# Graph-transformer kernel on one core: node rows kept in SBUF, three row buffers in the edge stage, seam flags moved

## The reference, cut to what matters

```python
h = maximum(layernorm(x), 0)
for l in range(2):
    k, q, v = typed_linear(h, ntype, Wk[l] / Wq[l] / Wv[l])          # per node
    a = (rel_apply(k[src], etype, Watt) * q[dst]).sum(-1) * pri / sqrt(16)
    alpha = segment_softmax(a, dst)                                 # 8 heads
    agg = segment_sum(alpha * rel_apply(v[src], etype, Wmsg), dst)
    out = silu(typed_linear(agg, ntype, Wa[l]))
    h = layernorm(out * sigmoid(skip[ntype]) + h * (1 - sigmoid(skip[ntype]))) * g[l] + b[l]
out = x + h @ Wff + bff
```

## Time and profile before

| | |
|---|---|
| median of 3 runs | 2857.04 us (2856.57 to 2858.19) |
| the profiled execution | 2860.01 us, span 2858.3 us |
| lists and tables | 0 to 198.8 us |
| node stage 0 | 198.8 to 378.8 us |
| edge stage, layer 0 | 378.8 to 1395.5 us |
| node stage 1 | 1395.5 to 1651.8 us |
| edge stage, layer 1 | 1651.8 to 2667.1 us |
| node stage 2 | 2667.1 to 2858.3 us |

### The profile page before, as it was taken

How to read it: one execution, slowest core, us unless ns; L and a number is a source line. 1 busy time by engine, 2 the same in 40 slices (tenths; PEclk the granted TensorE clock), 3 DMA queues, 4 the chain that set the end, 5 groups by cost and what they waited for, 6 DMA issues and landing times. The chain is left out here.

```text
span 2858.3 us, 54019 instructions
## 1 busy us (share of the span) xinstructions
PE 1898.7 (66%) x12612; PEld 1687.8 (59%) x12612; DVE 2161.5 (76%) x5507; ACT 1511.1 (53%) x5157; POOL 1966.4 (69%) x2064
## 2 busy tenths in 40 slices
PE   1857747677676766667577746777776776776466
PEld 1745536666666666666455546666666666666344
DVE  7987757778787878777477767777787877787388
ACT  0016725555555555555577725555555555555455
POOL 3706667777777777777277777777777777776176
PEclk6559977887788878887688968778778778787655
DMA  5719976666666666666467866666666666665611
GB/s 135 103 55 367 360 240 190 181 187 185 183 183 183 185 184 186 185 185 174 117 248 295 308 193 184 186 183 186 186 183 183 183 184 183 184 186 147 163 44 38
DMA packets 427424, 529.88 MB, mean 185 GB/s; under 512 B 71242, under 2 KB 342156, under 8 KB 414613
## 3 DMA queue, kind: packets, MB, share of 16 engines
q0 software_dynamic: 102144, 327.28, 37.1%
q1 hardware_dynamic: 315864, 197.40, 23.9%
q10 hardware_dynamic: 9104, 1.86, 0.4%
HBM read 393.41 MB, written 150.71 MB: 190 GB/s over the span
## 5 line engine op out<-in xcount | busy, mean ns | idle before, releaser
L1265 POOL DMA_INDIRECT g_rows<-node_kv,g_ids x1568 | 1485.0, 947 | 475.9 <-issue 452.7
L1528 PE MATMUL g_ps_q<-g_qw,g_hot_t 128*128 128x128 f32 x3136 | 589.0, 354 | 84.4 <-DMA g_qw<-node_q 51.4
L1448 ACT ACTIVATE acc<-acc,g_gained,g_scale x1568 | 601.0, 383 | 3.2 <-issue 2.2
L1528 PEld LDWEIGHTS g_ps_q<-g_qw,g_hot_t 128*128 128x128 f32 x3136 | 540.3, 262 | 97.3 <-DMA g_qw<-node_q 52.7
L1444 ACT ACTIVATE acc<-g_ps_sum 128x127 f32 x1568 | 412.1, 263 | 330.8 <-DVE g_gained L1375 270.5
L1509 PE MATMUL g_ps_sum<-g_hot,g_rows 128*128 128x128 f32 x3136 | 554.2, 331 | 4.0 <-ACT acc L1448 3.7
L1509 PEld LDWEIGHTS g_ps_sum<-g_hot,g_rows 128*128 128x128 f32 x3136 | 509.4, 244 | 13.7 <-ACT acc L1448 8.0
L1298 DVE TENSOR_TENSOR g_rows<-g_rows,g_ps_q 128x512 f32<-128x512 f32 x448 | 274.3, 613 | 289.1 <-DMA g_rows<-node_kv,g_ids 247.2
L1517 PE MATMUL g_ps_hot<-ident,g_hot_t 128*128 128x128 f32 x1568 | 289.7, 309 | 3.7 <-ACT g_hot L1453 3.6
L1453 ACT ACTIVATE g_hot<-g_ps_hot 128x512 f32<-128x512 f32 x448 | 233.4, 521 | 55.6 <-PE g_ps_hot L1517 55.6
L1517 PEld LDWEIGHTS g_ps_hot<-ident,g_hot_t 128*128 128x128 f32 x1568 | 231.5, 169 | 8.7 <-ACT g_hot L1453 4.6
(11 more groups left out here) (248 smaller groups left out, 3274.1 us busy)
## 6 DMA issues: line engine op xcount, KB each, us to landing
g_qw<-node_q SPq DMA_DIRECT2D x1568, 64.0 KB
g_rank_row<-edge_rank SPq DMA_DIRECT2D x114, 448.0 KB
g_rows<-node_kv,g_ids POOLq DMA_INDIRECT x1568
node_h<-n_norm SPq DMA_DIRECT2D x112, 64.0 KB
n_h<-node_h SPq DMA_DIRECT2D x14, 512.0 KB, 7.7
node_agg<-n_agg SPq DMA_DIRECT2D x24, 256.0 KB, 3.4
node_rows<-node_x SPq DMA_DIRECT2D x2, 1792.0 KB
node_q<-l_blank_q SPq DMA_DIRECT2D x1, 3200.0 KB
```

Of the source, the lines that this page charges most:

```text
L1265: g_.indirect_dma_start(out=rows[j][:, g, :], out_offset=None, in_=scratch["kv"][:, :], in_offset=bass.IndirectOffsetOnAxis(ap=ids[half][: ...
L1448: a.activation(at, at, ACT.Identity, scale=scale[j % 2][:, 0, g:g + 1], bias=gained[k % 2][:, g % FOUR:g % FOUR + 1]).then_inc(s["joined"], 1)
L1528: ins = t.matmul(ps_q[k % 2][:, n, :], hot_t[j % 2][:, g, :], qw[j % 2][:, g, :], start=True, stop=True)
```

## The change

- **h in SBUF.** A tensor `tab["h"]` of 128 x 56 x 128 floats stays in SBUF through the program. Stage 0 writes its normalised rows there, PE transposes them from there, and stages 1 and 2 read, mix and normalise them in place. The store and load of `node_h`, the buffers `n_norm` and the waits for both are gone. The six big work arrays of `edge_tables` lie in the same memory before.
- **Tables.** The ranks are kept as `tab["ranks"]` in bf16 and read back from the bf16 copy in HBM; the store of the f32 ranks is gone. The wait for those 14 DMAs moves from DVE to the end of SP's list. One copy (`e_lo_t`, L565) moves from DVE to ACT. `through` and `apart` are gone; the edge stage compares `pass` with 0 in two operations that take the place of L1350 and L1351.
- **Flags.** DVE makes the seam flags in node stage 0, a quarter of them in each of steps 10, 20, 30 and 40.
- **Edge stage.** U is 3. There is one buffer of ranks, so that SP loads the ranks of batch b+1 when the one-hots of batch b are made, before it goes on to the windows of batch b+1. The numbers of gathered rows are copied for 3 batches at a time (no copy after the last turn). The batches are written out by tables (`SIZES`, all 14), with the same order of work on each engine.

```diff
-U = 4
+U = 3
 # edge_tables
-        start, cid, rank, keyf, lo, hi = (sb(f"e_{n}", [Q, W]) for n in (...))
+        start, cid, rank, keyf, lo, hi = (tab["h"][0:Q, k * K7:(k + 1) * K7, :].rearrange("p t d -> p (t d)") for k in range(6))
-                sp.dma_start(scratch["rank"].rearrange("(p w) -> p w", w=W), rank[:, :]).then_inc(s["stored"], 16)
-                rank_d = scratch["rank"].rearrange("(b g o e) -> g o b e", g=G, e=P, o=1)
+                rank_d = scratch["rank16"][0:EP].rearrange("(b g o e) -> g o b e", g=G, e=P, o=1)
                 for g in range(G):
-                    sp.dma_start(lrb[g * H:(g + 1) * H, :, :], rank_d[g].to_broadcast([H, B, P])).then_inc(s["lrb_in"], 16)
+                    sp.dma_start(tab["ranks"][g * H:(g + 1) * H, :, :], rank_d[g].to_broadcast([H, B, P])).then_inc(s["lrb_in"], 16)
+                sp.wait_ge(s["lrb_in"], 16 * G)
-                did(v.tensor_copy(tiles_of(lo_t[:, :]), ps_t[1][:, 0:K7, 0:Q]))
-                dve.wait_ge(s["lrb_in"], 16 * G)
-                then(v.memset(tab["seam"][:, :, :], 0.0))
-                then(v.tensor_tensor(tab["seam"][:, :, 1:P], lrb[:, :, 1:P], lrb[:, :, 0:P - 1], ALU.subtract))
-                did(v.tensor_scalar(tab["seam"][:, :, 1:P], tab["seam"][:, :, 1:P], -BIG, None, ALU.mult))
-                then(v.tensor_scalar(tab["through"][:, :], tab["pass"][:, :], 0.0, None, ALU.is_equal))
-                did(v.tensor_scalar(tab["apart"][:, :], tab["through"][:, :], -1.0, 1.0, ALU.mult, ALU.add))
+            @block.scalar
+            def _(act):
+                act.wait_ge(s["pe"], 3)
+                nc.scalar.activation(tiles_of(lo_t[:, :]), ps_t[1][:, 0:K7, 0:Q], ACT.Copy).then_inc(s["lows"], 1)
 # node_stage
-                    for n in range(LOADS):
-                        load(h[:, n * TL:(n + 1) * TL, :], tiles(scratch["h"], n), rows_in[n])
-                        load(scratch["h"][n * P:(n + 1) * P, :], norm[n % NQ][:, :], h_out[n % NQ])
-                    a.activation(norm[i % NQ][:, :], xr[:, i, 0:D], ACT.Relu, bias=off[:, i:i + 1], scale=rstd[:, i:i + 1])
+                    a.activation(h[:, i, :], xr[:, i, 0:D], ACT.Relu, bias=off[:, i:i + 1], scale=rstd[:, i:i + 1])
+FLAG_STEPS = (10, 20, 30, 40)
+                def flags(k):
+                    part = slice(k * B // 4, (k + 1) * B // 4)
+                    of, ranks = tab["seam"][:, part, :], tab["ranks"][:, part, :]
+                    v.memset(of[:, :, 0:P + 1:P], 0.0).then_inc(s["flag_ends"], 1)
+                    v.tensor_tensor(of[:, :, 1:P], ranks[:, :, 1:P], ranks[:, :, 0:P - 1], ALU.subtract).then_inc(s["flag_steps"], 1)
+                    dve.wait_ge(s["flag_steps"], k + 1)
+                    v.tensor_scalar(of[:, :, 1:P], of[:, :, 1:P], -BIG, None, ALU.mult).then_inc(s["flag_ends"], 1)
 # edge_stage: SP, POOL, DVE
-        rank_row = [sb(f"rank_row{u}", [P, G * P], BF16) for u in range(2)]
+        rank_row = sb("rank_row", [P, G * P], BF16)
-                    if not early(b, 1):
-                        sp.wait_ge(s["hot_t"], b)
-                    ranks(b + 1, 1 - u)
+                    if b + 1 < BATCHES:
+                        sp.wait_ge(s["hot_t"], b + 1)
+                        ranks(b + 1)
-                        if g % FOUR == 0 and not early(b, U):
-                            pool.wait_ge(s["sums"], (b - U) * NF + g // FOUR + 1)
+                        if g % FOUR == 0 and b >= U:
+                            pool.wait_ge(s["sums"], GROUP[b - U] + g // FOUR + 1)
-                    v.tensor_tensor(coeff[:, :], grown[:, 0, :], tab["through"][:, bass.ds(b * G, G)], ALU.mult)
-                    v.tensor_tensor(add[:, :], grown[:, 1, :], tab["apart"][:, bass.ds(b * G, G)], ALU.max)
+                    v.scalar_tensor_tensor(out=coeff[:, 0:n], in0=tab["pass"][:, at:at + n], scalar=0.0, in1=grown[:, 0, 0:n], op0=ALU.is_equal, op1=ALU.mult)
+                    v.scalar_tensor_tensor(out=add[:, 0:n], in0=tab["pass"][:, at:at + n], scalar=0.0, in1=grown[:, 1, 0:n], op0=ALU.is_lt, op1=ALU.max)
```

More of the change, by code:

```diff
@@ L917, in step @@
                         rows_out(i, 3)
+                    if first and i in FLAG_STEPS:
+                        flags(FLAG_STEPS.index(i))
                     if real(i + 8) and not first:
@@ L1371, in gains @@
                     dve.wait_ge(s["scale_sb"], b + 1)
[L1372 to L1375 removed]
+                    dve.wait_ge(s["sums"], q + 1)
+                    if q >= 2:
+                        dve.wait_ge(s["joined"], UNTIL[q - 2])
@@ L1420, in _ @@
                 dve.wait_ge(s["zeroed"], 4)
-                one_hot(0, 0, 1)
-                def end():
-                    for n in range(U + 2):
-                        step(B // U - 1, n, B - U + n)
-                over(step, end, B - U)
+                one_hot(0)
+                over(step, 2)
             @block.scalar
@@ L1432, in _, with means @@
                 regs = [act.alloc_register(f"act_window{l}_{k}") for k in range(4)]
[L1434 to L1440 removed]
+                def means(b, k):
+                    q = GROUP[b] + k
+                    for n, g in enumerate(FOURS[b][k]):
+                        w, tile = windows(act, regs, b, g), FIRST[b] + g
+                        if n == 0:
+                            act.wait_ge(s["gained"], q + 1)
+                        if tile == 0:
@@ L1491, in end, with step @@
-                def end():
-                    for n in range(2):
-                        step(B // U, n, B + n)
-                over(step, end)
+                    of_batch = tab["seam"][first:first + m, FIRST[b] // G, :]
+                    a.activation(seam[0:m, :], of_batch, ACT.Copy).then_inc(s["flags"], 1)
+                    a.activation(same[0:m, :], of_batch, ACT.Relu, bias=c["ones"][first:first + m, 0:1]).then_inc(s["flags"], 1)
+                def step(b):
+                    new, mid, old = in_flight(b)
+                    has = lambda batch, k: batch is not None and k < len(FOURS[batch])
+                    if mid is not None:
+                        act.wait_ge(s["shifted"], mid + 1)
+                        a.activation(exp_t[0:SIZES[mid] * H, :], shifted[0:SIZES[mid] * H, :], ACT.Exp).then_inc(s["exp_t"], 1)
+                    if has(old, 0):
+                        means(old, 0)
+                    if has(new, 0):
+                        turned(new, 0)
+                    if has(old, 1):
+                        means(old, 1)
+                    if mid is not None:
+                        act.wait_ge(s["below"], 2 * mid + 2)
+                        a.activation(grown[:, :, 0:SIZES[mid]], below[:, :, 0:SIZES[mid]], ACT.Exp).then_inc(s["grown"], 1)
+                    if has(new, 1):
+                        turned(new, 1)
+                    if has(old, 2):
+                        means(old, 2)
+                    if has(new, 2):
+                        turned(new, 2)
+                    if mid is not None:
+                        act.wait_ge(s["scale_ps"], mid + 1)
+                        a.activation(scale[mid % 2][:, :, 0:SIZES[mid]], scale_ps[:, 0:2 * SIZES[mid]].rearrange("p (a g) -> p a g", a=2), ACT.Copy).then_inc(s["scale_sb"], 1)
+                    if has(old, 3):
+                        means(old, 3)
+                    if has(new, 3):
+                        turned(new, 3)
+                    if new is not None:
+                        flags(new)
```

483 lines of the change are left out of this document (212 added, 271 removed).

## The result

The changed kernel takes 2823.9 us (median of 4 runs, 2821.4 to 2825.0), the kernel before beside it 2856.8 (2856.3 to 2858.2). The ratio is 0.988, 95% interval 0.986 to 0.989. The prediction was 2822, -34.9 by its sum. The total came out; the parts did not all. The second traces are those of experiments 5 and 9.

A forecast was written before the change was run, and what follows sets the result against it. POOL's gather issue was taken to bound the edge stages, the DMA engines node stage 0. Terms -13.8 - 9 - 4 - 10 + 1.9 = -34.9 took the profiled 2860.01 to 2825.1, or 2822 us from the median 2857.04; range 2810 to 2834.

The forecast's parts named there:

- Tables, -13.8: Table stage: flags and two tables moved out, one copy given to ACT; 13.8 us gained (12 to 15).
- the 12.7 us: End of the tables: node stage 0 starts at 186.1 without the flags and two tables there, 12.7 us gained.
- by packets: SP's rank loads: half the bytes in as many packets, so they still take 53 us, not 27 by bytes.
- a load twice as long, my rival: Tables: 256-byte rank loads take 106.9 us, SP becomes last, node stage 0 starts at 206; 2842 us, chance 0.05.
- Node stage 0, -9: Node stage 0: relief from dropping h traffic, less the cost of the flags; -9 us (+1 to -14).
- I take 11 of the 14: Node stage 0: DMA relief without h is worth 14 us, of which 11 counted because the chain's floor is near.
- cost 2 us (0 to 10): Flags in node stage 0: four 2.5 us hiccups on DVE, mostly hidden by queued transfers; 2 us lost.
- The rival that I had given 0.11: Node stage 0: chain plus flags set the pace, the flags' 10 us paid in full; 2832 to 2840 us, chance 0.11.
- Node stage 1, -4: Start of node stage 1: without h loads, less gather latency and fewer POOL buffer waits; -4 us (0 to -9).
- Node stage 2, -10: Start of node stage 2: small loads issue 11.3 us earlier, so DVE starts sooner; -10 us (-7 to -13).
- Edge stages, +1.9: Both edge stages: POOL's row-number copies go from 15 to 19 a stage; +1.9 us, the other edits there 0.
- the price of the rival: Edge stages: three row buffers hold POOL, sums 6 us late cost 0.7 us a batch, +82; 2904 us, chance 0.07.

The follow-up runs named there:

- experiments 5 and 9: Both kernels run again unchanged for second traces: the changed kernel 2823.5 us (ratio 0.987), then the kernel before 2861.1 us.
- experiment 1: Changed kernel with the flags made whole in the table stage again, from bf16 ranks: 2824.1 us, ratio 0.987.
- experiments 2 and 10: Changed kernel with SP also storing h to DRAM in node stages 0 and 1, unread, run twice: 2828.3 us (ratio 0.989) and 2826.3.
- experiment 8: Changed kernel with seven unread 512 KB loads on SP's queue at the start of node stages 1 and 2, no stores: 2837.2 us.
- Experiment 12: Changed kernel with each group of gathers waiting for the sums two groups further on than its buffer needs: 3253.4 us.

## Why the prediction was right in its total and wrong in a term

**Tables, -13.8; measured -15.0 (right).** The end of the tables gave 18.72 - 4.92 = 13.8 us in the first traces: the flags and the two tables, and 1.0 because PE's slot matmuls took 3.86 us instead of 4.85, at a granted clock of 0.81 from 180 to 182 us against 0.50 before (the lower of its two levels, 1.2 GHz). The copy given to ACT brought the counting loop forward as forecast; 0.84 us more had come before it, with the load of the keys landing earlier (56.81 against 57.65), and the second trace of the changed kernel ends its tables 1.3 us later. That this last part is chance is likely, not shown. The forecast gave the 12.7 us to the move of the flags, and there it was wrong: by experiment 1 the same flags from bf16 ranks, left in the table stage, cost only 1 to 2 us of it. Most of the gain is that of their form. SP was never near being last. The loads went by their bytes, 28.35/53.44 = 0.53 of the time for half of them, so my choice of "by packets" was on the safe side and wrong. The Trainium skill's page "DMA: Bandwidth & Descriptors", section "Specifications", wants 512 bytes for line rate; a load twice as long, my rival, does not show here. While the loads ran (77.2 to 105.4 us), SP's queue had this row (packets, MB, share of 16 engines), and in the kernel before, from 77.4 to 130.8 us, the one below:

```profile
q1 hardware_dynamic: 5081, 1.30, 47.5%
```

```profile
q1 hardware_dynamic: 5258, 2.66, 46.6%
```

So about as many packets of 256 bytes went in half the time of those of 512, at the same share of the engines.

**Node stage 0, -9; measured -2.5, and -2.7 over four traces (wrong).** The step that failed is the sum "I take 11 of the 14" and "cost 2 us (0 to 10)". I took the relief against a floor of 55 x 2.63 = 145 us, from one undisturbed interval; without h and flags the puts span 158 to 160. Of the 13 to 15 us between, 9.4 to 10.4 stand at each fourth tile, where DVE loads registers. The kernel before has them as well (10.6 and 9.7), so the end of the landing waits could not win them back. So the relief is 7.0, not 11. And I took the flags as hidden under queued transfers. They put four stalls of 1.04 to 1.12 us on the puts, though a quarter is 1.74 us long and not 2.5. With h stored the other intervals give that back: ACT and DVE wait 34 and 35 us for landings in experiments 2 and 10, where the kernel before had 45 and 41 in a stretch as long; without it there is little to give back, and they cost 4.2 us. Each of the two edits took away the other's cover. The rival that I had given 0.11, that chain and flags eat the relief, is what happened for the most part; its 10 us for the flags was too high. The puts came 3.01 and 2.93 us apart, not the 2.8 that I had named as a sign.

**Node stage 1, -4; measured -7.5 (mis-sized).** 3 us are the loads, by experiment 8. 2.1 lie ahead of the first gather, where sums are stored at 345 GB/s instead of 285, which I hadn't foreseen; 1 to 2 us after the first put are inside what repeats vary by.

**Node stage 2, -10; measured -11.4 (right).** First gather to first output fell from 37.2 and 38.0 us to 28.2 and 27.8, 9.6 on the mean, and the faster stores of the sums gave the other 2.2. The loads in SP's queue bring 6.9 of the 9.6 back when they stand there again; the other 2.7 are open. Two readings were off. The limit that I named, DVE's first weights brought from 2700.10 to the row at 2688.94, gives 11.2 and not 10.6. And the row itself did not stay: it comes 2.5 us later after its gather than before, so DVE was ready 3.0 us ahead of it, and not within the 2 us that I had named. Without the faster stores, which I had not foreseen, the stage would have gained about 9.

**Edge stages, +1.9; measured -0.2 (nothing that shows).** The four more copies of row numbers in a stage are there and add 0.8 us of POOL's time; gathers and gaps vary by as much between traces. Three row buffers cost nothing, as forecast. But the price of the rival was wrong: I divided a delay of the sums by three batches. Experiment 12 shows that a delay beyond the margin counts whole in every batch, 4.0 us of 4.5, because the sums of batch b-3 are only made in the step that waits for the rows of batch b-1. At the 6 us that I had named the kernel would have lost 2.6 us a batch, some 290 and not 82. And the gain would be gone at sums about 3.7 us late, not 4.7. (Both are estimates from the median margin of 3.41: 6 less 3.4 in 112 batches, and 3.4 with the 0.31 of gain a batch.) The single rank buffer and the two fused comparisons, which I put at 0, were never run by themselves; these lengths show only that no sum of them stands out.

So a forecast of -34.9 met -35.6 in the spans of the two profiled executions (and -33 in the medians), because a term 6.5 us too large stood against four that were 1 to 3.5 too small. That the total fits so closely is luck. Stage 1's sign and most of stage 2 rest on the mechanism forecast; in the tables the serial path did shorten as read, but most of that came from cheaper flags and not from their move. Open: why the stores of the sums run faster in the changed kernel. Neither the loads nor the stores of h bring it back (14.1 and 13.7 us to the first gather with the loads, 14.0 with the stores), nor does PE's clock. It could be where the arrays lie in DRAM or SBUF; this was not tried.

## What to carry to other kernels

When two limits lie close together, price an edit against the kernel as it will be and not as it is: what hides a stall now may be what the same change removes. A floor read from one undisturbed interval is too low where something recurs at each fourth tile; take the whole period, and look at the queue's own instructions behind an "issue" wait. The price of a late buffer is found by asking in which step its release is made, not by the number of buffers.

## What the runs showed of the hardware

A load of node types into DVE's registers takes nearly as long for one register as for four (895 and 948 ns medians in node stage 0, 305 and 343 in node stage 2), while 14 at once took 1.3 to 6.0 us. So the load of four is nearly three times as long in stage 0 as in stage 2. What makes it so (the puts move over 300 GB/s there) was not tried. The Trainium skill's page "DMA: Bandwidth & Descriptors", section "Latency and other measured facts", gives a floor of some 600 ns for such a load; the rows here lie on both sides of it.

Between two traces of the same kernel a stage of DMA puts can differ by 4.5 us (180.0 and 175.5), with the whole within 1 us (spans 2822.7 and 2821.9). A term of that size needs more than one trace on each side.
